# Segment attention in a three-part decoder layer: the output projection as full-height three-term f32r matmuls, with token chunks split by parity over the partition halves

## The reference

```python
def proj(W, dh):
    p = jnp.einsum('bnld,df->bnlf', xs, W)
    return p.reshape(Bx, n_seg, H, L, dh).transpose(1, 0, 2, 3, 4)
def step(carry, qkv):
    mem, zc = carry
    qs, ks, vs = qkv
    sq = jax.nn.elu(qs) + 1.0
    mem = mem + jnp.einsum('bhsk,bhsv->bhkv', sq, vs)
    zc = zc + (jax.nn.elu(ks) + 1.0).sum(axis=-2, keepdims=True)
    scores = jnp.einsum('bhsk,bhtk->bhst', qs, ks) * scale
    att_dot = jnp.einsum('bhst,bhtv->bhsv', jax.nn.softmax(scores, axis=-1), vs)
    num = jnp.einsum('bhsk,bhkv->bhsv', sq, mem)
    den = sq.sum(axis=-1, keepdims=True) * zc
    att = gate * (num / den) + (1.0 - gate) * att_dot
    out_seg = att.reshape(Bx, L, H * DV) @ Wo
```

## Time and profile before

| | |
|---|---|
| median of 3 executions | 1859.03 us (1856.13 to 1859.97) |
| the profiled execution: its own time | 1858.56 us |
| its span | 1856.8 us |
| PE busy | 1766.6 us, 95% of the span |
| ACT, DVE, POOL busy | 82%, 78%, 38% |
| segment attention | from the start to about 797 us |
| one iteration of it (from one `attend` of unit 1 to the next) | 47.6 us |

### The profile page before, as it was taken

How to read it: one execution, slowest core, us unless ns; L and a number is a source line. 1 busy time by engine, 2 the same in 40 slices (tenths; PEclk the granted TensorE clock), 3 DMA queues, 4 the chain that set the end, 5 groups by cost and what they waited for, 6 DMA issues and landing times. The chain is left out here.

```text
span 1856.8 us, 43125 instructions
## 1 busy us (share of the span) xinstructions
PE 1766.6 (95%) x16161; PEld 1204.3 (65%) x16262; DVE 1443.2 (78%) x2685; ACT 1527.4 (82%) x4485; POOL 705.4 (38%) x810
## 2 busy tenths in 40 slices
PE   6999999999999999899999999999999999999995
PEld 5888888888888888758999998722222222222244
DVE  6677777777777777546666666699999999999957
ACT  6777777777777777737888885699999999999977
POOL 2334334433444444403766650033332332333325
PEclk9999999999999999999999999999999999999998
DMA  7333333322332333442011005833354345335102
GB/s 171 57 60 62 67 59 61 66 61 60 61 64 62 63 59 53 84 128 83 20 41 46 16 13 111 252 47 46 54 75 56 47 62 76 46 46 72 21 1 91
DMA packets 140591, 121.65 MB, mean 66 GB/s; under 512 B 78923, under 2 KB 112607, under 8 KB 140383
## 3 DMA queue, kind: packets, MB, share of 16 engines
q1 hardware_dynamic: 140383, 118.88, 33.3%
HBM read 77.29 MB, written 41.53 MB: 64 GB/s over the span
## 5 line engine op out<-in xcount | busy, mean ns | idle before, releaser
L2080 DVE TENSOR_REDUCE s_neg_max<-x_psum 128x1 f32<-128x1024 f32 x512 | 579.9, 1217 | 1.5 <-PE x_psum L1967 1.5
L2012 ACT ACTIVATE s_prob<-x_psum,s_neg_max 128x1024 f32<-128x1024 f32 x512 | 570.4, 1115 | 1.7 <-DVE s_neg_max L2080 0.7
L1984 PE MATMUL x_psum<-s_prob,s_v_norm 128*32 128x256 f32 x4096 | 325.7, 391 | 1.0 <-DVE s_v_norm L2089 1.0
L1967 PE MATMUL x_psum<-f_stack 128*128 128x512 bf16 x923 | 286.5, 383 | 27.2 <-issue 17.7
L2054 POOL TENSOR_TENSOR s_row_inv<-s_row_sum,s_neg_one 128x4 f32<-128x4 f32 x127 | 128.0, 1008 | 394.7 <-ACT s_prob L2012 394.7
L612 POOL TENSOR_SCALAR a_relu_ring<-a_qT 128x512 f32<-128x512 f32 x64 | 98.7, 1559 | 344.2 <-ACT a_qT L479 316.9
L1984 PEld LDWEIGHTS x_psum<-s_prob,s_v_norm 128*32 128x32 f32 x4096 | 81.3, 108 | 216.5 <-issue 213.9
L1967 PEld LDWEIGHTS x_psum<-f_stack 128*128 128x128 bf16 x1024 | 58.4, 97 | 231.1 <-ACT s_prob L2012 223.2
L508 ACT ACTIVATE a_prob<-a_psum,a_neg_max 128x128 f32<-128x128 f32 x512 | 179.8, 400 | 21.4 <-DVE a_neg_max L728 21.4
L771 DVE SCALAR_TENSOR_TENSOR a_att<-a_psum,a_keep_cols,a_num_s 128x128 f32<-128x128 f32 x256 | 72.1, 345 | 133.0 <-ACT a_num_s L534 125.9
L1328 ACT ACTIVATE x_prob<-x_psum,x_neg_max 128x77 f32<-128x77 f32 x512 | 161.2, 340 | 15.9 <-DVE x_neg_max L1486 15.8
(11 more groups left out here) (209 smaller groups left out, 4122.5 us busy)
## 6 DMA issues: line engine op xcount, KB each, us to landing
f_stack<-qk_thirds SPq DMA_DIRECT2D x256, 128.0 KB, 6.9
segment_values<-a_v_stage SPq DMA_DIRECT2D x64, 256.0 KB, 3.2
a_v_pos<-segment_values SPq DMA_DIRECT2D x512, 32.0 KB
qk_thirds<-p_third SPq DMA_DIRECT2D x16, 768.0 KB, 8.4
a_x_in<-in_x_dram SPq DMA_DIRECT2D x16, 256.0 KB, 3.4
a_x_res<-in_x_dram SPq DMA_DIRECT2D x32, 128.0 KB, 2.8
after_attention<-a_normed SPq DMA_DIRECT2D x32, 128.0 KB, 2.4
x_x_in<-after_attention SPq DMA_DIRECT2D x32, 128.0 KB, 2.1
```

The costliest lines, as they stand in the source:

```text
L1967: last = pe.matmul(ring[n % 3][:, f * HALF:(f + 1) * HALF], k_stack[:, slot, j, kt * P:(kt + 1) * P], q_stack[:, slot, j, f * HALF:(f + 1) ...
L1984: last = pe.matmul(acc[32 * j:32 * j + 32, s], v_norm[:, step // KT % 2, step % 4, j, :], prob[:, step % 4, j, s], start=step % (2 * KT) = ...
L2012: act.activation(prob[:, step % 4, j, :], ring[n % 3], ACT.Exp, bias=neg_max[:, step % 2, j:j + 1], accum_out=row_sum[:, step % 4, j:j + 1 ...
L2080: dve.tensor_reduce(neg_max[:, step % 2, j:j + 1], ring[n % 3], AX_X, ALU.max, negate=True).then_inc(max_ready, 1)
```

## The change

1. **Projection at full height.** For each iteration `project_out` now runs per segment t over 8 chunk pairs; each is three f32r matmuls of 128 rows and 256 columns: hi x hi, hi x lo and lo x hi. The weights are split once at the start into `w_out_hi` and `w_out_lo` (ACT and POOL), from a place that the Wv load used first.
2. **Parity on the partition halves.** Partition half q now holds the chunks of parity q. So each matmul of `attend` is cut into two of 64 columns (8 chunks of 8 elements), and there are 16 for num and 16 for pv. num and pv of head half e share bank 5 + e, so ACT now waits for `pv_done`, and `attend(u)` waits at its start for `att_ready` of unit u-1.
3. **Eight small instructions for four.** `scale_num` and `combine` have 8 instructions of 128x64 each per unit; `combine` writes in place into `num_s`, and that of unit 3 moves into the next preparation.
4. **The split of att.** Two new steps per unit: `high_att` on ACT (a copy of 128x512 rounded to f32r) and `low_att` on POOL (a subtraction of 128x512). `project_out` and `scale_num` wait for `att_low`.
5. `z_gate` is written by 4 instructions instead of 1; the residual, the normed rows and their DMAs are by segment; the gates are loaded for all 16 heads on both halves; banks 4 and 5 swap roles in places.

```diff
-TURN_BANK, NUM_BANK, PV_BANK, X_BANK = bank[4], bank[5], bank[6], bank[7]
-Y_BANK = (bank[5], bank[6])
+TURN_BANK, X_BANK = bank[4], bank[7]
+Y_BANK = (bank[4], bank[6])
 def project_out(pe, it, t, chunks):
     if chunks[0] == 0:
-        pe.wait_ge(att_ready, 4 * it + 4)
+        pe.wait_ge(att_low, 4 * it + 2 * t + 2)
+        if t == 0:
+            pe.wait_ge(probT_ready, 8 * it + 8)
     for c in chunks:
-        for e in range(2):
-            last = pe.matmul(Y_BANK[e][:, 0:D], att[rows(e), c, :, :].rearrange("p m i -> p (m i)"),
-                             w_out[rows(e), c, :], start=c == 0, stop=c == H - 1, skip_group_check=True)
+        hi, lo = (part[:, c, t, :, :, :].rearrange("p e g i -> p (e g i)") for part in (att_hi, att_lo))
+        for n, (left, right) in enumerate(((hi, w_out_hi), (hi, w_out_lo), (lo, w_out_hi))):
+            last = pe.matmul(Y_BANK[t][:, 0:D], left, right[:, c, :], start=c == 0 and n == 0,
+                             stop=c == H // 2 - 1 and n == 2, skip_group_check=True)
...
 def attend(it, u):
-    pe.wait_ge(phiT_ready, 4 * it + max(u, 1) + 1)
+    pe.wait_ge(phiT_ready, 4 * it + 4)
     pe.wait_ge(mem_added, 4 * it + u + 1)
-    if u > 0:
-        pe.wait_ge(num_scaled, 4 * it + u)
-    for gi in range(4):
-        for e in range(2):
-            last = pe.matmul(NUM_BANK[rows(e), gi * P:(gi + 1) * P], mem[rows(e), t, g, :],
-                             phiT[rows(e), t, g, :], start=True, stop=True)
-    last.then_inc(num_done, 1)
-    pe.wait_ge(probT_ready, 8 * it + 2 * u + 2)
     if u > 0:
         pe.wait_ge(att_ready, 4 * it + u)
+    for gi in range(4):
+        for e, q in ((0, 0), (1, 1), (0, 1), (1, 0)):
+            last = pe.matmul(num(e, gi)[rows(q), :, :],
+                             mem[rows(e), t, g, :], chunk_half(phiT[rows(e), t, g, :], q),
+                             start=True, stop=True)
+    pe.wait_ge(probT_ready, 8 * it + 2 * u + 2)
     for gi in range(4):
         for e in range(2):
-            last = pe.matmul(PV_BANK[rows(e), gi * P:(gi + 1) * P], v_pos[:, it % 2, t, e * GR + half * 4 + gi, :],
-                             probT[:, e, gi, :], start=True, stop=True)
+            for q in range(2):
+                last = pe.matmul(pv(e, gi)[rows(q), :, :],
+                                 v_pos[:, it % 2, t, e * GR + half * 4 + gi, :],
+                                 chunk_half(probT[:, e, gi, :], q), start=True, stop=True)
     last.then_inc(pv_done, 1)
...
 def scale_num(it, u):
-    act.wait_ge(num_done, 4 * it + u + 1)
+    act.wait_ge(pv_done, 4 * it + u + 1)
     act.wait_ge(zgate_ready, it + 1)
     if it * 4 + u >= 2:
-        act.wait_ge(att_ready, 4 * it + u - 1)
-    for gi in range(4):
-        g = half * 4 + gi
-        last = act.mul(num_s[:, u % 2, gi, :], NUM_BANK[:, gi * P:(gi + 1) * P],
-                       z_gate[:, it % 2, t, g:g + 1])
+        act.wait_ge(att_low, 4 * it + u - 1)
+    for e in range(2):
+        for gi in range(4):
+            last = act.mul(sums(u, e, gi), num(e, gi), z_gate[:, it % 2, t, e, g:g + 1])
...
+def high_att(it, u):
+    act.wait_ge(att_ready, 4 * it + u + 1)
+    act.copy(in_unit(att_hi, u), by_chunk(num_s[:, u % 2, :])).then_inc(att_high, 1)
...
+def low_att(it, u):
+    pool.wait_ge(att_high, 4 * it + u + 1)
+    pool.tensor_tensor(in_unit(att_lo, u), by_chunk(num_s[:, u % 2, :]),
+                       in_unit(att_hi, u).bitcast(F32), ALU.subtract).then_inc(att_low, 1)
+pool.wait_ge(w_high, 7)
+pool.tensor_tensor(w_out_lo[:, :, :].rearrange("p a b -> p (a b)"), stage[WV],
+                   w_out_hi[:, :, :].rearrange("p a b -> p (a b)").bitcast(F32), ALU.subtract
+                   ).then_inc(wo_low, 1)
 for it in range(ITER):
     for u in range(UNITS):
+        if u == 3 and it > 0:
+            low_att(it - 1, 3)
         relu_q(it, u)
...
     normalise(it, 3)
+    for u in range(UNITS - 1):
+        low_att(it, u)
```

187 lines of the change are left out of this document (113 added, 74 removed).

## The result

The changed kernel takes **1897.9 us** (median of 4 runs, 1896.7 to 1899.2) against 1859.5 for the kernel before on the same chip (4 runs, 1856.1 to 1860.4): a ratio of 1.0211, 95% interval 1.0198 to 1.0223. It is slower, by 2%. The forecast was 1908, range 1868 to 1932. PE is TensorE, ACT is ScalarE, DVE is VectorE and POOL is GpSimd.

The account below looks back on a forecast made before the run. PE, busy 47.38 of 47.61 us an iteration, was taken to pace the stage. Attention +48.6, preparation -8.3, last iteration +5.0 and start +4 gave +49.3 on 1858.56: 1908 us, range 1868 to 1932.

Parts of the forecast that it names:

- The hand-off waits: PE waiting for ACT's copy before turns: 1.78 us after unit 2, 0.38 after 1, 0.55 after 0; +2.68 together.
- p: Cost of one small ACT scaling instruction: 0.20 us at 64 columns, ends 0.15 and 0.25.
- `attend`: PE's num and pv with 64-column matmuls, both priced as the memory update: 2.04 to 2.18 us, +0.56 an iteration.
- Rival B: Four 64x64 tiles run at once in num: 0.55 to 0.76 us instead of 1.09, about 1880; chance 0.22.
- The preparation: Stretch between attention parts: projection saves PE 1.89 us, some 1.3 returns as waits and hand-overs; -0.55 an iteration.
- what went back: In the preparation, waits of 0.5, 0.35 and 0.3 us plus hand-over times return some 1.3 of 1.89.
- The last iteration: No projections cover the waits: a unit goes from 4.03 to 5.65 us, with the last `attend` +5.0.
- C: Hand-off waits are covered and the kernel is faster, 1848 us; gains if p is below 0.144; chance 0.07.
- D: Small ACT instructions have a floor, p = 0.25; preparation saves nothing, whole start counts: 1939 us; chance 0.11.
- The projection's rate: Projection on PE: 48 f32r matmuls of 256 columns at 0.117 us each, 5.62 instead of 7.51.
- The start: Weight split on ACT and POOL ahead of the first relu, 8.8 us, about half absorbed: +4 (0 to +9).
- The last projection: End of the stage: the last projection ends 8.7 us after the last `attend`, before and after; adds nothing.

Follow-up runs that it names:

- The version with VectorE: Changed kernel with the scaling of units 0 to 2 moved from ACT to VectorE, two broadcast-gate instructions per unit: 1851.9 us, ratio 0.9953 to the kernel before.
- the filler: Changed kernel plus ten unread identity matmuls per unit of the last iteration, between the first and second turn: 1892.7 us, ratio 1.0176 to the kernel before.

## Why the prediction held, point by point

- **The hand-off waits: right, in size and place.** 1.79, 0.40 and 0.57 measured, 1.78, 0.38 and 0.55 forecast, out of rows of three different instruction kinds. p was 0.1975 for 0.20. The version with VectorE gave back 2.70 of 2.76 per iteration.
- **`attend`: the term that was wrong.** "For num, four 64x64 tiles in turn, no row shows it": it was priced as the memory update, 1.09, and took 0.62; pv took 1.09 as forecast, `attend` 1.71. That is 0.47 a unit, 1.88 an iteration; 1.70 of it shows in the attention part, which grew by 1.54 for a forecast of 3.24, 26 us in 15 iterations. Rival B named the mechanism, and its 0.55 to 0.76 holds the measured 0.62. What was held against it (two of the tiles share their rows) did not weigh: the pairs took 0.90, the fours 0.62. The Trainium skill ("TensorEngine Tiling (Array Packing)", Tiling Modes) has four independent 64x64 tiles in parallel; the trace agrees in kind, and the measured 0.62 lies between its halving of 1.09, 0.55, and the forecast of B from the earlier trace rows, 0.76.
- **The kernel did not come out at B's 1880** because two other terms went the other way. The preparation: -0.55 forecast, +0.24 measured, 12 us. In the forecast's terms two thirds of that is the projection itself, whose blocks saved 1.36 and not 1.89, and one third what went back, 1.60 for 1.3. The waits were looked for before the third scores (0.5), the projection of segment 1 (0.35) and the fourth turn (0.3), and stood before the second turn (0.75, where it had "just in time") and the fourth (0.79). `low_att` was cheaper than priced (1.28 for 1.57), but ACT's Q copies, which release the chain, ended only 0.43 before `attend` and not 1.1, in part since the shorter num brought that end forward by 0.47; what makes up the rest is not shown. And less work on PE gave nothing here: with 3.7 fewer still the preparation stayed as long, in part by the clock.
- **The last iteration: right in sign, wrong in make-up.** +8.4 for +5.0. Of that 6.1 is the 1.2 GHz level, which the forecast had not in it and which the filler took away; it made the period 6.64 instead of 5.38 and the last projection's end later. Without it the growth is 2.3: the forecast took three distances of 4.03 for the kernel before, and the first of them, from 773.00 to 778.42, was 5.42. Two errors of opposite sign met here too.
- **Rivals C and D fell.** For C p would have had to be under 0.144, for D 0.25. The sum of the idle times before the turns was 2.76 per iteration, not under 1.
- **The projection's rate: right for a long block, too low for short ones.** 24 matmuls in 2.85, 12 in 1.50 and 6 in 0.90 are 0.119, 0.125 and 0.15 each with their start, for the row's 0.117, which was read from the middle of a block.
- **The start**: +3.75 for +4, in traces whose starts differ by up to 3 us with the same code up to there. **The last projection**: the sum forecast nothing; from the last `attend` it ended 2.0 later, inside the 8.4 above, and 0.4 earlier with the clock held up.
- **The sum** is 39.1 for 49.3: -26 by num, +12 by the preparation, +3.4 by the last iteration. That 1898 lies only 10 from the forecast is luck: errors of both signs met, and num's alone would have made it 1882, near B's 1880. The range would have held that too. The forecast's direction rested on the hand-off waits, which were right.

What stays open: how much of the preparation's length would remain if relu and phi never overlapped; no run separates them. And which of num's two properties, row half or column half, carries the gain from pairs to fours.

## What to carry to other kernels

When a dependency is moved later, count on the engine that serves it what stands between the release and the consumer, instruction by instruction; here eight small ones of 0.2 us in front of one copy, waiting for a later event than before, made 2.6 us of new waits an iteration and outweighed the 1.4 that the projection saved on the engine that was 95% busy. Before splitting a per-partition scale into more pieces, see whether an idle engine can do all of it in one instruction with a broadcast operand: that alone turned the change from 2% slower to 0.5% faster. Work taken off the busiest engine can be worth nothing in a stretch that another pair of engines sets, and can lower its clock.

## What the runs showed of the hardware

- 16 float32 matmuls (32 records) of 64 rows and 64 columns into four 64x64 tiles in rotation: 0.62 us; in pairs: 0.90; 16 of 128 rows (32 records) into two column halves: 1.09.
- With waits of 1.36 per unit in the last iteration, the granted clock was 0.51; with ten idle matmuls in each wait it was 0.99, and the kernel 6 us faster for more work. In the preparation, with two thirds of the projection removed, it was 0.66 in a window where it had been 1.00.
- VectorE's phi took 0.68 to 0.71 alone, 1.01 when it started just behind the start of a relu on GpSimd (which kept its 1.47), and 1.36 to 1.45 when it started within 0.4 of the start of a subtraction or a normalisation there. A relu that started while a phi ran took 1.79 to 1.93. All are 128x512. In these rows it is the one that starts second that is stretched.
- One VectorE instruction of 128x256 out of PSUM with a gate broadcast over two dimensions takes 0.38; four of ACT's, of 128x64 each, for the same columns take 0.79.
